# A vision tower whose last mixture of experts works on rows sorted by expert in device memory

## What is computed

```
def _L1_ffn_ref(x, gate_w, gate_b, w1, b1, w2, b2):
    B, S, H, E, K = (8, 1024, 128, 8, 2)
    logits = jnp.einsum('bsh,he->bse', x, gate_w) + gate_b
    topk_vals, topk_idx = jax.lax.top_k(logits, K)
    topk_weights = jax.nn.softmax(topk_vals, axis=-1)
    mask = jax.nn.one_hot(topk_idx, E, dtype=topk_weights.dtype)
    weights = jnp.einsum('bske,bsk->bse', mask, topk_weights)
    h = jax.nn.relu(jnp.einsum('bsh,ehf->bsef', x, w1) + b1)
    expert_out = jnp.einsum('bsef,efh->bseh', h, w2) + b2
    return jnp.einsum('bseh,bse->bsh', expert_out, weights)
...
h = h + _L0_attn_ref(_layernorm(h, axis=-1), ...)
h = h + _L0_ffn_ref(_layernorm(h, axis=-1), ...)
h = h + _L1_attn_ref(_layernorm(h, axis=-1), ...)
h = h + _L1_ffn_ref(_layernorm(h, axis=-1), ...)
```

## Time and profile before

| | |
|---|---|
| median of 3 runs | 2148.41 us (2145.86 to 2150.23) |
| the profiled execution's own time | 2147.26 us |
| its span, first to last instruction | 2145.4 us |
| PE busy over the span | 94% |
| last stage, `dense_mixture` | 1597.5 to 2145.4 us, 547.9 us |
| `attention` a0 | from 332 us to 876 us |
| `layer_norm` f0, with the load of `rest` | 886 to 922 us |

### The profile page before, as it was taken

How to read it: one execution, slowest core, us unless ns; L and a number is a source line. 1 busy time by engine, 2 the same in 40 slices (tenths; PEclk the granted TensorE clock), 3 DMA queues, 4 the chain that set the end, 5 groups by cost and what they waited for, 6 DMA issues and landing times. The chain is left out here.

```text
span 2145.4 us, 68990 instructions
## 1 busy us (share of the span) xinstructions
PE 2006.2 (94%) x27049; PEld 1536.5 (72%) x27049; DVE 1146.2 (53%) x3516; ACT 1036.3 (48%) x3106; POOL 629.5 (29%) x866
## 2 busy tenths in 40 slices
PE   6999997899999998789988999999979999999999
PEld 2444445667667766477756888888749999999998
DVE  0000036777777777466664555555455555555555
ACT  0000035565555555444455555555455555555555
POOL 0000004777777777201102343443300000000000
PEclk9999999999999999969999999999989999999999
DMA  8677700000000000200000000000000000000000
GB/s 319 270 290 298 297 14 2 4 3 3 3 3 3 3 3 4 89 1 1 1 1 2 2 2 2 2 2 2 2 1 9 9 7 8 7 7 9 7 9 9
DMA packets 22329, 91.81 MB, mean 43 GB/s; under 512 B 5093, under 2 KB 13549, under 8 KB 15597
## 3 DMA queue, kind: packets, MB, share of 16 engines
q1 hardware_dynamic: 20302, 86.00, 10.3%
q10 hardware_dynamic: 1822, 2.68, 0.4%
HBM read 84.41 MB, written 4.26 MB: 41 GB/s over the span
## 5 line engine op out<-in xcount | busy, mean ns | idle before, releaser
L1383 ACT ACTIVATE hidden_m<-ps,s_f_b 128x128 f32<-128x128 f32 x1040 | 296.3, 368 | 224.4 <-PE ps L1326 220.8
L808 PE MATMUL ps<-xn,s_a_wqkv 128*128 128x260 f32 x1024 | 289.3, 406 | 11.5 <-ACT qk_a L554 7.4
L1326 PE MATMUL ps<-xn,s_f_w 128*128 (+1 forms) x2080 | 286.5, 282 | 1.4 <-ACT hidden_m L1383 1.4
L153 PE MATMUL ps<-x_chunk,s_w_tok 128*128 128x512 f32 x576 | 253.0, 598 | 21.4 <-DMA s_cls<-in_cls 21.4
L1462 DVE SCALAR_TENSOR_TENSOR acc_m<-ps,weights_m,acc_m 128x128 f32<-128x128 f32 x520 | 182.3, 351 | 151.0 <-ACT acc_m L1406 102.0
L1326 PEld LDWEIGHTS ps<-xn,s_f_w 128*128 128x128 f32 x2080 | 254.1, 193 | 9.4 <-ACT hidden_m L1383 1.6
L1338 PE MATMUL ps<-s_f_w,hidden_m 128*128 128x128 f32 x2080 | 253.6, 275 | 0.0
L1338 PEld LDWEIGHTS ps<-s_f_w,hidden_m 128*128 128x128 f32 x2080 | 242.6, 192 | 1.6
L153 PEld LDWEIGHTS ps<-x_chunk,s_w_tok 128*128 128x128 f32 x576 | 108.8, 191 | 163.7 <-issue 142.4
L808 PEld LDWEIGHTS ps<-xn,s_a_wqkv 128*128 128x128 f32 x1024 | 176.1, 192 | 57.9 <-ACT qk_a L554 20.2
L1312 POOL COPY xn_tile_m<-xn 128x128 f32 (+1 forms) x65 | 19.1, 293 | 536.0 <-PE ps L1365 494.2
(11 more groups left out here) (196 smaller groups left out, 4165.3 us busy)
## 6 DMA issues: line engine op xcount, KB each, us to landing
x_chunk<-in_x_main SPq DMA_DIRECT2D x48, 1536.0 KB, 9.4
out<-acc_m SPq DMA_DIRECT2D x65, 64.0 KB, 1.5
s_f_w<-in_f_w SPq DMA_DIRECT2D x2, 1024.0 KB
x_chunk<-in_x_tail SPq DMA_DIRECT2D x16, 96.0 KB, 12.5
s_w_tok<-in_w_tok ACTq DMA_DIRECT2D x1, 1216.0 KB, 9.4
s_a_wqkv<-in_a_wqkv ACTq DMA_DIRECT2D x1, 768.0 KB
s_a_wqkv<-in_a_wqkv SPq DMA_DIRECT2D x1, 768.0 KB
s_f_w<-in_f_w SPq DMA_DIRECT2D x2, 256.0 KB
```

Source lines behind the costliest of these rows:

```text
L153: nc.tensor.matmul(ps[:, a.slot, :], w_tok[:, k, :], xb[:, a.slot, k, :], start=(k == 0), stop=False)
L808: nc.tensor.matmul(ps[:, QK_BANK[i], 0:QUAD], w_qkv[:, c * P:(c + 1) * P], xn[:, t.h * QUAD:(t.h + 1) * QUAD], start=True, stop=True).then ...
L1326: last = nc.tensor.matmul(ps[:, b % 2, i * P:i * P + n], w1[:, c * P:(c + 1) * P], xn[:, bass.ds(a.index * n, n)], start=True, stop=True)
L1383: last = nc.scalar.activation(hid[:, a.slot, c, :], ps[:, b % 2, i * P:i * P + n], ACT.Relu, bias=b1[:, c:c + 1])
```

## The change

`dense_mixture` is replaced by `sparse_mixture`, and two earlier stages get work for it.

1. Device memory holds two tensors of "expert rows", one for the first choices and one for the second (k = 0, 1). In each, every expert has a region of 8448 rows of 130 numbers (the token's 128 features, its name, its weight). Before use they are filled with padding rows, whose name is a row behind the real ones. `fold_first` makes the pattern on POOL (`pad`), and 37 transfers from SP write it at the start of `attention` a0 (`pads`).
2. Part one of the new stage runs over 13 groups of 5 tiles. PE makes logits, turns `xn` into rows, counts with bf16 matmuls how many tokens before this one chose the same expert, and makes residual rows; DVE chooses (`choose`) and works out each token's row in its expert's region (`seat`); POOL sends 10 indirect transfers a group, each scattering 128 rows of 520 bytes by a list of row numbers; SP stores the residual rows to `acc` in device memory.
3. Then a table gives, for each of 41 blocks of 256 rows per choice, the first row of the block and the column of its expert's weights. 41 blocks are enough for any division of the tokens; blocks without real rows are computed as well.
4. Part two runs over 2 x 41 = 82 blocks. SP reads the block's row number into a register and loads the block; PE reads the column number into a register, turns the block, multiplies by w1, turns the result, multiplies by w2; ACT and DVE copy between; POOL adds each half block of 128 rows to `acc` with an indirect transfer that adds. There are 8 input buffers and 4 output buffers. Before block 41 POOL waits until all adds of the first choices have landed.
5. At the end SP waits for all adds and copies `acc` to `out`, 4.26 MB from device memory to device memory.

```diff
+REGION = 33 * 256
+ROW = D + 2
+BLOCK_ROWS = 256
...
+        if later:
+            @block.sync
+            def _(sp):
+                for dst, src in later:
+                    sp.dma_start(dst, src).then_inc(later_in, 16)
...
+    T = 5
+    GN = T * P
+    G = tokens // GN
+    K = 2
+    NB = tokens // BLOCK_ROWS + E1 + 1
+    RING, YS = 8, 4
...
+            for g in range(G):
+                sp.wait_ge(base_sb, 2 * g + 2)
+                sp.dma_start(acc[g * GN:(g + 1) * GN, :].rearrange("(t p) d -> p t d", p=P), base[:, g % 2])\
+                    .then_inc(acc_in[g % 2], 16)
+            sp.wait_ge(table_done, 1)
+            for i in range(3):
+                sp.wait_ge(sent[i], 16 * K * T * len(range(i, G, 3)))
+            for b in range(total):
+                row = sp.value_load(row_i[0:1, b // NB, b % NB:b % NB + 1], min_val=0,
+                                    max_val=REGION * E1 + BLOCK_ROWS * (E1 - 1))
+                if b >= RING:
+                    o = b - RING
+                    sp.wait_ge(added[o % YS], 32 * (o // YS + 1))
+                sp.dma_start(blk[:, b % RING], regions[b // NB][bass.ds(row, BLOCK_ROWS), :]
+                             .rearrange("(h p) c -> p h c", p=P)).then_inc(loaded[b % RING], 16)
...
+            pool.wait_ge(pads_in, pads)
+            for g in range(G):
+                pool.wait_ge(slot_done, g + 1)
+                pool.wait_ge(xt_sb, 2 * g + 2)
+                for t in range(T):
+                    for k in range(K):
+                        nc.gpsimd.indirect_dma_start(
+                            regions[k][:, :], bass.IndirectOffsetOnAxis(ap=slot_i[:, g % 3, t, k:k + 1], axis=0),
+                            rows[:, g % 3, t, 2 * k:2 * k + ROW], None).then_inc(sent[g % 3], 16)
...
+                for half in range(2):
+                    pool.wait_ge(y_done, 2 * b + half + 1)
+                    nc.gpsimd.indirect_dma_start(
+                        acc[:, :], bass.IndirectOffsetOnAxis(
+                            ap=blk[:, b % RING, half, name_of(b):name_of(b) + 1].bitcast(I32), axis=0),
+                        ys[:, b % YS, half, :], None, compute_op=ALU.add).then_inc(added[b % YS], 16)
...
+            def up(b):
+                columns[b % 2] = pe.value_load(col_i[0:1, b // NB, b % NB:b % NB + 1], min_val=0,
+                                               max_val=F1 * (E1 - 1))
+                pe.wait_ge(bt_sb, b + 1)
+                since(pe, hs_sb, b - 1)
+                for half in range(2):
+                    last = nc.tensor.matmul(ps[:, 1 + b % 2, half * F1:(half + 1) * F1],
+                                            xt[:, b % 2, half * P:(half + 1) * P],
+                                            w1[:, bass.ds(columns[b % 2], F1)], start=True, stop=True)
+                last.then_inc(up_ps, 1)
...
+            turn_block(0)
+            for b in range(total + 1):
+                if b < total:
+                    up(b)
+                if b + 1 < total:
+                    turn_block(b + 1)
+                if b >= 1:
+                    down(b - 1)
+                if b < total:
+                    turn_hidden(b)
...
+                nc.scalar.activation(hs[:, b % 2], ps[:, 1 + b % 2, 0:2 * F1].rearrange("p (i f) -> p i f", f=F1),
+                                     ACT.Copy).then_inc(hs_sb, 1)
...
+                for f in range(2):
+                    nc.scalar.activation(hid[:, b % 2, f, :],
+                                         ps[:, 3 + b % 2, f * BLOCK_ROWS:(f + 1) * BLOCK_ROWS], ACT.Relu,
+                                         bias=bias[:, b // NB, b % NB, f:f + 1]).then_inc(hid_sb, 1)
...
+            nc.gpsimd.memset(pad[:, :, :, :], 0.0).then_inc(pad_done, 1)
...
-        dense_mixture(nc, tokens, h, xn, ps, S["ident"], S["f1_gate"], S["f1_gate_b"], S["expert_ids"],
-                      S["f1_w1"], S["f1_b1"], S["f1_w2"], S["f1_b2"], out)
+        sparse_mixture(nc, tokens, h, xn, ps, S["ident"], S["before"], S["all_ones"], S["f1_gate"], S["f1_gate_b"],
+                       S["expert_ids"], S["f1_w1"], S["f1_b1"], S["f1_w2"], S["f1_b2"], regions, acc, pads_in,
+                       16 * len(pads), out)
```

More of the change, by code:

```diff
@@ L1262, in dense_mixture @@
[L1262 to L1271, removed]
@@ new lines, in sparse_mixture @@
+        limit = sb("limits_m", [P, K, E1, NB - E1])
+        over = sb("over_limit_m", [P, K, E1, NB - E1])
+        blocks = sb("blocks_of_m", [P, K, E1])
+        upto = sb("not_after_m", [P, E1, E1])
+        part = sb("prefix_terms_m", [P, K, E1, E1])
+        end = sb("end_block_m", [P, K, E1])
+        number = sb("block_number_m", [P, NB])
+        past = sb("past_m", [P, K, NB, E1])
+        gone = sb("gone_m", [P, K, NB, E1])
+        expert = sb("block_expert_m", [P, K, NB])
+        first = sb("blocks_before_m", [P, K, NB])
@@ L1304, in _ @@
+            for i in range(YS):
+                sp.wait_ge(added[i], 32 * len(range(i, total, YS)))
+            sp.dma_start(out[:, :].rearrange("(a b) d -> a (b d)", a=P),
+                         acc[0:tokens, :].rearrange("(a b) d -> a (b d)", a=P)).then_inc(stored, 16)
+            sp.wait_ge(stored, 16)
         @block.gpsimd
         def _(pool):
[L1306 to L1313, removed]
@@ L1316, in _ @@
         @block.tensor
         def _(pe):
[L1318 to L1340, removed]
-                last.then_inc(y_ps, 1)
@@ L1343, in step @@
[L1343 to L1370, removed]
-                if a:
-                    up(a, 3)
@@ new lines, in ranks @@
+            def ranks(g):
+                pe.wait_ge(chosen_done, g + 1)
+                since(pe, carry_done, g)
+                nc.tensor.matmul(rank_at(), before[:, :], chosen[:, g % 2], start=True, stop=False)
+                for i in range(T):
+                    last = nc.tensor.matmul(rank_at()[:, i + 1:T + 1], all_ones[:, :],
+                                            chosen[:, g % 2, i:i + 1].to_broadcast([P, T - i, K, E1]),
+                                            start=False, stop=(i == T - 1))
+                last.then_inc(rank_ps, 1)
@@ new lines, in _, with turn_block @@
+            logits(0)
+            turn_x(0)
+            for g in range(G):
+                ranks(g)
+                if g + 1 < G:
+                    logits(g + 1)
+                    turn_x(g + 1)
+                turn_weights(g)
+                bases(g)
+            columns = [None, None]
+            def turn_block(b):
+                pe.wait_ge(loaded[b % RING], 16 * (b // RING + 1))
+                since(pe, bt_sb, b)
+                for half in range(2):
+                    last = nc.tensor.transpose(ps[:, 0, half * P:(half + 1) * P], blk[:, b % RING, half, x_of(b)],
+                                               ident[:, :])
+                last.then_inc(bt_ps, 1)
@@ new lines, in _ @@
+            for g in range(G):
+                choose(g)
+                seat(g)
+            dve.wait_ge(carry_done, G)
+            chained(nc.vector.tensor_tensor(over[:, :, :, :], carry[:, :, :].unsqueeze(3)
+                                            .to_broadcast([P, K, E1, NB - E1]), limit[:, :, :, :], ALU.is_gt))
+            settle()
+            chained(nc.vector.tensor_reduce(blocks[:, :, :], over[:, :, :, :], AX.X, ALU.add))
+            settle()
+            for k in range(K):
+                last = nc.vector.tensor_tensor(part[:, k], blocks[:, k, :].unsqueeze(1).to_broadcast([P, E1, E1]),
+                                               upto[:, :, :], ALU.mult)
```

460 lines of the change are left out of this document (333 added, 127 removed).

## The result

The changed kernel takes 2287.3 us (median of four runs, 2286.1 to 2292.7) against 2147.1 us: a ratio of 1.066, with an interval of 1.063 to 1.068. It is slower, where faster was forecast. They differ in how much `attention` a0 loses and in part one of the mixture, by 18 and 33 us; why they differ is open.

A forecast was written before the change was run, and what follows sets the result against it. The prediction took PE, busy 94% of the span, to bound the kernel. It summed 1597.5 ahead of the mixture, 3 outside and 466 for the new mixture to a 2066 us span, 2070 us on the median's scale, range 1985 to 2260.

The forecast's parts named there:

- Its cover is attention a0: Padding transfers: their 245 us would fit under `attention` a0, 525 us long with DMA share 0.01.
- I allow 2 us for those coming late: `attention` a0: the padding runs beside 104 packets, nearly all instruction code; late ones would cost 2 us.
- The price of a row: Padding transfers: a row would cost 27 ns of one engine, so 143,360 rows take 245 us.
- The rival of an overrun: Padding outlasting `attention` a0: at 100 ns a row 896 us, some 350 us more; chance 0.03.
- The rivals of the register read: Part two, PE's register read stalling longer: 1.5 us a block gives 2136 (0.10), 2.8 us gives 2243 (0.07).
- everything hiding: Mixture: scatters under 0.75 us and a register read taken early give 1958 us; chance 0.12.
- dear scatters: Mixture: scatters cost POOL 2.1 us (1.7 to 2.4), total 2264 us, slower than before; chance 0.26.
- A plain scatter: POOL in the mixture: 0.95 us of writing words at the memset's rate plus 0.29, 1.24 us; bounds 0.3 to 2.1.
- An adding scatter: POOL in part two: the same 1.24 us, two a block make 2.5 us, under PE's 3.2.
- The register read: PE in part two: 0.7 us a block on top of 2.5 us of work, making 3.2 us.
- Part one: Mixture: POOL bounds at 12.4 us a group, 161 us, over DVE's floor of 7.5 and PE's 5.2.
- The clock: PE in part two: a granted clock of 0.87 would add 0.37 us a block, 31 us, inside the range.

The follow-up runs named there:

- e1: The kernel before plus only the pad pattern in `fold_first` and the 37 padding transfers in `attention` a0, mixture still dense: 2312.3 us, ratio 1.075.
- e3: The kernel before plus the pad pattern, with the 37 padding transfers issued in `dense_mixture` and the stores of `out` moved to POOL: 2157.7 us.
- the second set: The changed kernel run again unchanged, five runs: 2231.5 us, ratio 1.038 against the kernel before.
- e8: The changed kernel with all 294 indirect transfers, and what waits for them, left out: 2082.7 us.
- e6: The changed kernel with only the padding that blocks can read, written in the mixture and none in `attention` a0: 2110.0 us, ratio 0.982 against the kernel before.

## Why the prediction was wrong

**The step that failed** is "Its cover is attention a0", with "I allow 2 us for those coming late". The price of a row was low (0.048 us against 0.027; the padding took 422 us and not 245), but it still fitted. What failed is the 2 us: measured 142 and 124 us, and 160 in e1. I had the row that carried the cause, 104 packets, nearly all of them code, in a stage of straight code, and put down 2 us for it without working it out. What counts is that PE stops when one is late: 24 times for 51 packets in the stretch of the padding, 82 us of gaps, and a lower granted clock on top. e3 shows that it is not the traffic as such. The rival of an overrun (0.03) was not it: the weights' loads came as before, and `layer_norm` f0 with them; the cover itself grew. The rivals of the register read and of everything hiding did not come either. That the second set's 2231.5 us lies in my range of 1985 to 2260 is luck: the slow end stood for dear scatters. The first set's 2287.3 lies outside.

**The mixture**, on the trace of the second set, term by term:

| term | forecast | measured |
|---|---|---|
| to the first scatter | 9 | 7.6 |
| part one on POOL | 161 | 164.6 |
| to the first add | 4 + 6 | 12.9 |
| part two | 262 + 3 | 306.1 |
| last adds and copy | 3 + 18 | 17.4 |
| sum | 466 | 508.6 |

- *A plain scatter*: 1.24 us forecast, 0.96 + 0.30 = 1.26 measured. The fixed cost of about 2.0 us that the Trainium skill gives for a transfer by GpSimd ("DMA: Bandwidth & Descriptors", "Anatomy of one DMA") does not stand in POOL's way: in this trace a scatter lands 2.3 us after its issue, and the next one starts 1.26 us after it. My working, words written at the memset's rate, no run confirms: with the same list an adding scatter holds POOL 1.55 us. The hit may be luck.
- *An adding scatter*: taken at the same 1.24, measured 1.86. This is the mis-sized term that made POOL the bound of part two: 164 x 1.86 = 305 us. The rival of dear scatters had the place right ("POOL without gaps in part two"), for half of them.
- *The register read*: 0.30 us long, and a block without transfers 2.71 us against my 2.5 + 0.7. The 600 ns of the Trainium skill ("DMA: Bandwidth & Descriptors", "Latency and other measured facts") are twice what this trace shows. PE's matmuls were as forecast.
- *Part one*: POOL was the bound, as forecast. The floor under it was not DVE's 7.5 us a group but PE, 6.2 us at a granted clock of 0.79 (e8), where I had 5.2.
- *The clock*: in the second set it was 0.59 in part one and 0.97 in part two, and POOL set the pace of both, so it is no term of this sum.
- *The pattern in `fold_first`*: 1 us forecast (the other 2 of my 3 were for late code), 3.2 measured. *The copy*: 15.0 us to landing, forecast 18.

With the padding at nothing and the mixture at 508.6, the span would be 1597.5 + 3 + 508.6 = 2109, and e6 had 2107.5. So the sparse form does gain, but about half of what I forecast: the mixture is 39 us shorter and not 82, and adding is 41 of the 43 us between. The padding lost that gain and more.

## What to carry to other kernels

A bulk transfer is not free because its stage issues no transfers: the engines of a stage of straight code load that code by DMA too, 98 packets here, and a late piece stopped PE for 2 to 8 us. Put bulk traffic beside loops, or make it small: here 12,288 rows written late did what 143,360 did early. And price each kind of POOL's transfers by itself: adding made one cost 1.86 us from start to start in place of 1.26.

## What was not expected of the hardware

- PE goes on 1.3 to 1.8 us after its code packet has ended, in each of 24 stalls.
- A 64 KB store on another queue lands after 8.7 us beside the padding, 1.8 us alone; DVE's `neg_max_a` keeps its median of 701 ns.
- A scatter of 128 rows costs POOL 0.96 us for 520 or 1032 bytes a row, 1.55 with adding, and 0.30 to the next.
- `attention` a0 loses 124 to 160 us to the same padding in different sets of runs, each set within 0.6%.
